# The LSTM steps of a graph and recurrent kernel: where the four gates of a half lie in PSUM, and when each is signalled to ScalarE

## The reference, cut to what matters

```python
x = x + segment_sum(support[src] * w, dst)     # graph layer on layernorm(x); 6250 nodes, 100000 edges
x = x + ffn(layernorm(x))                      # one sequence of 6250 places, 256 features

def step(carry, xp):                           # the LSTM inside ffn, once per place
    h, c = carry
    i, f, g, o = split(xp + h @ W_hh.T, 4)     # 256 columns each
    c = sigmoid(f) * c + sigmoid(i) * tanh(g)
    h = sigmoid(o) * tanh(c)
# after it: a gate per place (argmax of two logits), sums before and after each place,
# 2*h + prefix*fw + suffix*bw
```

## Time and profile before

| | |
|---|---|
| median of 3 runs | 1757.58 us |
| span of the profiled execution | 2362.0 us |
| its own time outside the span | not given |
| plain steps 50 to 113 in it | from 2033.8 us to about 2327 us |
| busy: TensorE, VectorE, GpSimd, ScalarE | 70%, 57%, 49%, 23% of the span |

### The profile page before, as it was taken

How to read it: one execution, slowest core, us unless ns; L and a number is a source line. 1 busy time by engine, 2 the same in 40 slices (tenths; PEclk the granted TensorE clock), 3 DMA queues, 4 the chain that set the end, 5 groups by cost and what they waited for, 6 DMA issues and landing times.

```text
span 2362.0 us, 35522 instructions
## 1 busy us (share of the span) xinstructions
PE 1644.3 (70%) x9417; PEld 1363.5 (58%) x9417; DVE 1357.8 (57%) x4075; ACT 532.0 (23%) x1838; POOL 1166.9 (49%) x1235
## 2 busy tenths in 40 slices
PE   5696766666664576576676676676776776889994
PEld 3385555555552365465565565565565555889993
DVE  8997787777763444344444444444443444556666
ACT  1121000000000022222221222221222222566662
POOL 0377556556545535444444444444344354027774
PEclk9898787878885778777777777787787777999997
DMA  6112222322222223223223223223232233233334
GB/s 169 35 43 61 72 73 68 99 71 73 71 64 80 80 81 93 84 71 95 82 76 95 78 78 94 76 84 93 71 93 84 71 94 101 89 115 114 113 113 131
DMA packets 71694, 202.43 MB, mean 86 GB/s; under 512 B 22785, under 2 KB 25046, under 8 KB 70773
## 3 DMA queue, kind: packets, MB, share of 16 engines
q0 software_dynamic: 48048, 116.84, 18.1%
q1 hardware_dynamic: 23600, 85.04, 11.1%
HBM read 160.49 MB, written 41.17 MB: 85 GB/s over the span
## 4 chain that ended last, share of the span: by engine, by line
PE 45%; issue 20%; DVE 20%; another core or an unknown queue 8%; DVEq 3%; ACT 3%; DMA 0%; POOL 0%; SPq 0%; ACTq 0%
PE bank L1642 14%; PE bank L1616 13%; PE bank L1635 7%; PE bank L1573 5%; PE bank L1540 3%; DVE big_a L999 3%; DVE big_b L1054 2%; DVE big_a L995 2%; DVEq L1057 2%; PE bank L1624 1%; DVE big_c L1048 1%; DVE big_c L997 1%; DVE listed L938 1%; DVE w_ih L938 1%
## 5 line engine op out<-in xcount | busy, mean ns | idle before, releaser
L538 POOL DMA_INDIRECT big_a<-support_scratch,stg_g x636 | 603.8, 949 | 692.2 <-ACT stg_g L618 513.8
L1054 DVE TENSOR_TENSOR big_b<-big_b,bank 125x256 f32 x881 | 367.1, 417 | 663.3 <-remote 396.6
L1642 PE MATMUL bank<-big_c 128*128 128x125 f32 x3648 | 520.8, 287 | 290.7 <-issue 247.9
L1642 PEld LDWEIGHTS bank<-big_c 128*128 128x128 f32 x3648 | 481.2, 199 | 325.4 <-issue 292.2
L1616 PE MATMUL bank<-big_a,big_c 128*125 128x256 f32 x1272 | 474.4, 479 | 122.6 <-issue 94.8
L1616 PEld LDWEIGHTS bank<-big_a,big_c 128*125 128x125 f32 x1272 | 258.6, 239 | 206.8 <-issue 182.4
L1048 DVE TENSOR_SCALAR big_c<-consts_sb,listed 128x125 f32<-128x125 f32 x881 | 308.2, 351 | 76.8 <-issue 49.5
L511 POOL DMA_INDIRECT big_a<-support_scratch,stg_g x245 | 233.9, 955 | 185.3 <-ACT stg_g L618 117.1
L1573 PE MATMUL bank<-big_a,big_c 128*125 128x256 f32 x490 | 171.9, 481 | 151.7 <-issue 91.1
L1635 PEld LDWEIGHTS bank<-xt,w_ih 128*128 128x128 f32 x1600 | 234.6, 213 | 26.0 <-ACT xt L592 10.3
L1635 PE MATMUL bank<-xt,w_ih 128*128 128x125 f32 x1600 | 235.9, 296 | 1.0 <-ACT xt L592 0.8
(11 more groups left out here) (238 smaller groups left out, 1695.0 us busy)
## 6 DMA issues: line engine op xcount, KB each, us to landing
big_c<-gate_input_scratch SPq DMA_DIRECT2D x64, 508.0 KB
gate_input_scratch<-pr SPq DMA_DIRECT2D x50, 508.0 KB
big_a<-support_scratch,stg_g POOLq DMA_INDIRECT x881
support_scratch<-pr SPq DMA_DIRECT2D x12, 448.0 KB
big_b<-in_x SPq DMA_DIRECT2D x2, 1904.0 KB
out<-big_a SPq DMA_DIRECT2D x2, 1456.0 KB
big_b<-in_x SPq DMA_DIRECT2D x1, 1792.0 KB
out<-big_a SPq DMA_DIRECT2D x1, 1344.0 KB
```

Source lines behind the costliest of these rows:

```text
L538: pool.indirect_dma_start(out=ring[:, s, :], out_offset=None, in_=sup_d, in_offset=bass.IndirectOffsetOnAxis(ap=stg_g[:, q, n:n + 1], axis ...
L1054: V.tensor_tensor(at, at, bank[4 + s % PSR][0:SEGS, 0:D], ALU.add).then_inc(added, 1)
L1642: return mm(bank[b + x][:, c * SEGS:(c + 1) * SEGS], w_hh[:, k, g:g + P], h_s[:, q, k, :], start=False, stop=True, skip_group_check=True)
```

## The change

For the plain steps, g leaves the bank of its half. i, f and o stay in the bank 2 - 2q + x (columns 125 to 500), and the two g (half 0 and half 1) share the bank 5 + q. In the far steps sigmoid(o) is written to columns 0 to 125 of the half's own gate bank, where g was. TensorE signals three times for each half: i and f ready (if_r), g ready (g_r), o ready (o_r), and ScalarE waits for each apart. Since ScalarE now reads a bank into which TensorE has still to write, TensorE waits for the reader: for a_if[0] ahead of the last product of o of half 0, for a_g[0] ahead of the last product of g of half 1, for a_if[1] ahead of the last product of o of half 1. `turn_back` is issued ahead of that very last product. Seeds are three copies: both g (250 columns), then i, f, o of each half (375 columns), the latter after h_r[x] of the step before the seeded bank is used anew. Step 49 runs all products in the order k, half, gate. `prefix` uses bank 4 instead of 5. Banks 5 and 6 are written once more before step 49.

```diff
-            def recur(u, q, extra=0, b=None):
-                b = 2 - 2 * q if b is None else b
-                pe.wait_ge(seeded[0], u + 1)
-                pe.wait_ge(seeded[1], u + 1)
+            def recur(u, q, extra=0, back_of=None):
+                pe.wait_ge(seeded_g, u - (SEGL - 1))
+                for x in range(2):
+                    pe.wait_ge(seeded[x], u + 1)
                 pe.wait_ge(h_r[0], u + (extra + 1))
                 for c in (1, 2, 0, 3):
-                    product(q, 0, 0, c, b)
-                for c in (1, 2):
-                    product(q, 0, 1, c, b)
+                    apart(q, 0, 0, c)
+                for c in (0, 1):
+                    apart(q, 0, 1, c)
                 pe.wait_ge(h_r[1], u + (extra + 1))
-                for c in (1, 2, 0, 3):
-                    ins = product(q, 1, 0, c, b)
-                ins.then_inc(g_r[0], 1)
-                for c in (0, 3):
-                    product(q, 0, 1, c, b)
-                for c in (1, 2, 0, 3):
-                    ins = product(q, 1, 1, c, b)
-                ins.then_inc(g_r[1], 1)
+                apart(q, 1, 0, 1)
+                apart(q, 1, 0, 2).then_inc(if_r[0], 1)
+                apart(q, 1, 0, 0).then_inc(g_r[0], 1)
+                for c in (2, 3):
+                    apart(q, 0, 1, c)
+                pe.wait_ge(a_if[0], u + 1)
+                apart(q, 1, 0, 3).then_inc(o_r[0], 1)
+                apart(q, 1, 1, 1)
+                apart(q, 1, 1, 2).then_inc(if_r[1], 1)
+                pe.wait_ge(a_g[0], u + 1)
+                apart(q, 1, 1, 0).then_inc(g_r[1], 1)
+                if back_of is not None:
+                    turn_back(back_of, q)
+                pe.wait_ge(a_if[1], u + 1)
+                apart(q, 1, 1, 3).then_inc(o_r[1], 1)
...
             for x in range(2):
                 pe.wait_ge(xe_r[x], SEGL)
-            for b in (2, 3):
+            pe.wait_ge(added, PSR + TILES)
+            for b in (2, 3, 5, 6):
                 ins = mm(bank[b][:, 0:4 * SEGS], rank_b[:], any_bits, start=True, stop=True)
             ins.then_inc(bits, 1)
-            recur(SEGL - 1, 1, 0, 0)
+            pe.wait_ge(seeded[0], SEGL)
+            pe.wait_ge(seeded[1], SEGL)
+            for k in range(2):
+                pe.wait_ge(h_r[k], SEGL)
+                for x in range(2):
+                    for c in range(4):
+                        ins = product(1, k, x, c, 0)
+                    if k == 1:
+                        ins.then_inc(g_r[x], 1)
```

On ScalarE:

```diff
-            def seed_loaded(u, pair, q, w):
+            def seed_loaded(u, pair, q, w, extra=0):
                 act.wait_ge(xp_l[q], pair * 16 - (SEGL // 2 * 16 - 16))
                 for x in range(2):
                     act.wait_ge(a_o[x], u - 1)
+                given = taken_in[q].rearrange("p (x c) k -> p x c k", x=2)
+                nc.scalar.copy(cell_home(q)[:, 0:2 * SEGS].rearrange("p (x k) -> p x k", x=2),
+                               given[:, :, 0, w:w + SEGS]).then_inc(seeded_g, 1)
                 for x in range(2):
-                    seed_half(q, x, w, 2 - 2 * q, taken_in)
+                    act.wait_ge(h_r[x], u + extra)
+                    nc.scalar.copy(gates_home(q, x)[:, SEGS:4 * SEGS].rearrange("p (c k) -> p c k", c=3),
+                                   given[:, x, 1:4, w:w + SEGS]).then_inc(seeded[x], 1)
...
+            def gates_apart(u, q, x, far):
+                g = gates_home(q, x)
+                i_f, o_g = homes(x, q, far)
+                act.wait_ge(if_r[x], u - (SEGL - 1))
+                nc.scalar.activation(i_f, g[:, SEGS:3 * SEGS].rearrange("p (c k) -> p c k", c=2),
+                                     ACT.Sigmoid).then_inc(a_if[x], 1)
+                act.wait_ge(g_r[x], u + 1)
+                nc.scalar.activation(act_g[:, x, :], cell_home(q)[:, x * SEGS:(x + 1) * SEGS], ACT.Tanh
+                                     ).then_inc(a_g[x], 1)
+                act.wait_ge(o_r[x], u - (SEGL - 1))
+                nc.scalar.activation(o_g, g[:, 3 * SEGS:4 * SEGS], ACT.Sigmoid).then_inc(a_o[x], 1)
```

More of the change, by code:

```diff
@@ L296, in build @@
         seeded = [sem(f"gates_seeded{x}") for x in range(2)]
+        seeded_g = sem("cell_gates_seeded")
         g_r = [sem(f"gates_ready{x}") for x in range(2)]
+        if_r = [sem(f"gates_i_f_ready{x}") for x in range(2)]
+        o_r = [sem(f"gate_o_ready{x}") for x in range(2)]
         a_if = [sem(f"act_i_f_done{x}") for x in range(2)]
@@ L326, in build, with gates_home, cell_home, homes @@
         STORES = (len(LEAVING) - 1) * 32
-        def homes(x, far):
+        def gates_home(q, x):
+            return bank[2 - 2 * q + x]
+        def cell_home(q):
+            return bank[5 + q]
+        def homes(x, q, far):
             if far:
                 return (bank[4][:, x * 2 * SEGS:(x + 1) * 2 * SEGS].rearrange("p (c k) -> p c k", c=2),
-                        bank[5 + x][:, 0:SEGS])
+                        gates_home(q, x)[:, 0:SEGS])
             return act_if[:, x, :, :], act_o[:, x, :]
@@ L676, in seed_loaded, with gates @@
                     act.wait_ge(a_o[x], u - 1)
+                given = taken_in[q].rearrange("p (x c) k -> p x c k", x=2)
+                nc.scalar.copy(cell_home(q)[:, 0:2 * SEGS].rearrange("p (x k) -> p x k", x=2),
+                               given[:, :, 0, w:w + SEGS]).then_inc(seeded_g, 1)
                 for x in range(2):
-                    seed_half(q, x, w, 2 - 2 * q, taken_in)
-            def gates(u, q, x, far, b=None):
-                g = bank[(2 - 2 * q if b is None else b) + x]
-                i_f, o_g = homes(x, far)
+                    act.wait_ge(h_r[x], u + extra)
[12 more added lines that the diff above has]
+                nc.scalar.activation(o_g, g[:, 3 * SEGS:4 * SEGS], ACT.Sigmoid).then_inc(a_o[x], 1)
+            def gates(u, q, x):
+                g = bank[x]
+                i_f, o_g = homes(x, q, False)
                 act.wait_ge(g_r[x], u + 1)
@@ L691, in tanh_c, with step @@
                 nc.scalar.activation(act_c[:, x, :], c_s[:, 1 - q, x, :], ACT.Tanh).then_inc(a_c[x], 1)
[L693 to L697, removed]
+            def step(u, q, far=False):
+                for x in range(2):
+                    gates_apart(u, q, x, far)
+                    tanh_c(u, q, x)
             def take_and_seed(u, q, w):
@@ L717, in place @@
                     for x in range(2):
-                        gates(u, q, x, False, 0)
+                        gates(u, q, x)
                     tanh_c(u, q, 0)
@@ L743, in _ @@
             seed_loaded(SEGL, SEGL // 2, 0, 1)
-            step(SEGL - 1, 1, False, 0)
+            for x in range(2):
+                gates(SEGL - 1, 1, x)
+                tanh_c(SEGL - 1, 1, x)
             seed_loaded(SEGL + 1, SEGL // 2, 1, 1)
@@ L767, in _ @@
                             take_input(j, q, x, j - 1)
+                act.wait_ge(bits, 3)
                 with act.Fori(0, slow_sweeps) as sweep:
@@ L770, in _ @@
                     for q in range(2):
[L771 removed]
+                        seed_loaded(u0 + q, m0, q, 2, sweep)
                     act.sem_inc(ago, 1)
@@ L1382, in finish @@
                 dve.wait_ge(o_v, outputs - 1)
-                link(V.tensor_tensor(base, bank[5][0:SEGS, D:2 * D], bw[0:SEGS, :], ALU.mult))
-                link(V.tensor_tensor(w_even, bank[5][0:SEGS, 0:D], diff, ALU.mult))
+                link(V.tensor_tensor(base, bank[4][0:SEGS, D:2 * D], bw[0:SEGS, :], ALU.mult))
+                link(V.tensor_tensor(w_even, bank[4][0:SEGS, 0:D], diff, ALU.mult))
                 link(V.tensor_tensor(base, base, w_even, ALU.add))
@@ L1643, in product, with apart @@
                           start=False, stop=True, skip_group_check=True)
-            def recur(u, q, extra=0, b=None):
-                b = 2 - 2 * q if b is None else b
-                pe.wait_ge(seeded[0], u + 1)
-                pe.wait_ge(seeded[1], u + 1)
+            def apart(q, k, x, c):
+                g = (4 * x + c) * P
+                home = cell_home(q)[:, x * SEGS:(x + 1) * SEGS] if c == 0 else gates_home(q, x)[:, c * SEGS:(c + 1) * SEGS]
+                return mm(home, w_hh[:, k, g:g + P], h_s[:, q, k, :], start=False, stop=True, skip_group_check=True)
@@ L1664, in place, with turn_back @@
+            def turn_back(n, q):
+                if not isinstance(n, int) or n > 0:
+                    pe.wait_ge(terms_r, n)
+                mm(bank[7][0:SEGS, 0:P + 1], h_s[:, q, 0, :], back[0], start=True, stop=True)
+                mm(bank[7][0:SEGS, P:2 * P + 1], h_s[:, q, 1, :], back[1], start=False, stop=True,
+                   skip_group_check=True).then_inc(back_r, 1)
             def place(it, q):
@@ L1748, in _ @@
             recur(WARM, 0)
-            recur(WARM + 1, 1)
-            turn_back(0, 1)
+            recur(WARM + 1, 1, 0, 0)
             with pe.Fori(1, SEGL // 2) as it:
[L1752 to L1755, removed]
```

(13 more changed lines are left out.)

5 lines of the change are left out of this document (2 added, 3 removed).

## The result

Before 1757.94 us (median of 5 runs), after 1747.76 us (5 runs, 1747.3 to 1750.41). The ratio is 0.9946, interval 0.9935 to 0.9957: 9.5 us saved, against 20.3 forecast. The direction was right, the time lies inside the range, but the gain is under half of what was forecast.

A forecast was written before the change was run, and what follows sets the result against it. The chain from TensorE's first ten products through ScalarE and VectorE to the next step, 4.56 us, was taken as the bound; 63 step starts x 0.33 = 20.8, less 0.5 net, gave 1737.3 us, range 1729.5 to 1750.5.

The forecast's parts named there:

- the last term of the period: TensorE, last o to next step: two loads at 0.11 us; two more waits hidden or costing up to 0.11.
- i and f signalled apart: Start of each plain step: i, f ready after 8 products instead of 10, first sigmoid at 2.13 us instead of 2.58.
- The handshake from ScalarE to TensorE: Held weight loads, such as the last o's: they start 0.05 to 0.11 us after the sigmoid they wait for.
- The rival on the slower side: Weight loads waiting for ScalarE: handshake 0.43 us instead of 0.05, period 4.83, time 1775 us; chance 0.08.
- Half 1 fits by a hair: Half 1's i, f product is ready at 3.57 us, ScalarE free at 3.58, so ScalarE sets the time.
- o behind a wait: Half 0's last product waits for a_if[0]: stream slips about 0.1 us, o ready at 3.13, before tanh(c) at 3.37.
- o in its own bank: Sigmoid of o writing into the bank it reads: taken as no cost; bounds nothing and a doubling, +0.28 us.
- The seeds: ScalarE's three copies instead of two: 1.09 us instead of 1.00, leaving 0.2 us of cover before the next sigmoid.
- Without outputs: Plain steps without outputs: TensorE idles about 0.5 us for a_if[1]; period 4.26 us, gain 0.33 a step.
- The rule of the semaphore increments: TensorE's signals: at 26.3 ns each, four more would add 0.105 us a step, 6.7 us, making 1744; judged unlikely.
- The signs that were named: Trace of plain steps: first sigmoid at 2.1 us, steps 4.2 to 4.3 apart, idle time moved before the last product.
- The first rival: ScalarE or small slips in plain steps take half the gain: period 4.35 to 4.50, 1749 us at 4.42; chance 0.15.

The follow-up runs named there:

- experiment 3: The kernel before the change with TensorE's two loops over the plain steps written out; 1759.1 us, ratio to before 1.0004.
- experiment 1: The changed kernel with TensorE's two loops over the plain steps written out, nothing else touched; 1735.86 us, ratio to before 0.9872.
- experiments 4 and 5: 4: the changed kernel with the turning back behind the last product of o instead of ahead; 1759.3 us, ratio 1.0004. 5 has its own line.
- experiment 5: The changed kernel with TensorE's loops kept, each body begun mid-step behind the product that signals g_r[0]; 1737.35 us, ratio to before 0.9877.

## Why the prediction was wrong

The step that failed is the last term of the period: "the next step's load is due behind them", 0.11 us, with up to 0.11 for two more waits. It counted TensorE's engine instructions and its waits, and not what TensorE's sequencer does between two steps: a branch and register values, which no row of an engine's timeline lists. From the last o's first load to the next step's it reckoned two loads at 0.11, with that allowance 0.22 to 0.33. In one step in two it is 0.30, which the term covers. In the other it is 0.64: 0.34 more, and 0.37 in the steps without outputs. The trace has 23 such intervals with outputs and 6 without (the last pass of a loop does not go back), and 0.2 us more at the loops' ends: 23 x 0.34 + 6 x 0.37 + 0.2 = 10.2 us. From the first sigmoid of step 50 to that of step 113 the kernel after takes 277.7 us and experiment 3 288.0. So 10.3 us are gained in the traces, where 20.8 were forecast, and 20.8 - 10.2 = 10.6; the timed runs have 9.5 (7.6 to 11.4). The prediction said of the two new waits that they "can hide behind the last two matmuls". Two matmuls are 0.22 us; the branch, which it did not count, is 0.21 alone.

The other steps, point by point:
- *i and f signalled apart*: right. From a step's first load to its sigmoid it is 2.09 us (1607.14 to 1609.23), where 2.13 was forecast. In experiment 1 the interval is 4.18 with outputs, between the 4.17 and 4.23 of the text.
- *The handshake from ScalarE to TensorE*: sigmoid of half 1 ends at 1601.85 + 0.36 = 1602.21, the load it holds begins at 1602.26. That is 0.05, the low bound. The rival on the slower side falls with it.
- *Half 1 fits by a hair*: right; its sigmoid starts 1.46 after that of half 0 (1600.39, 1601.85), as before.
- *o behind a wait*: right. Sigmoid of o waits for TensorE (0.38 us) and tanh(c) still follows in time (1602.78, 1603.08).
- *o in its own bank*: nothing, as taken. 259 ns by the group below, where the earlier trace rows had 276.

```profile
L704 ACT ACTIVATE bank<-bank 128x125 f32<-128x125 f32 x99 | 25.6, 259 | 38.3 <-PE bank L1676 38.3
```

- *The seeds*: 1603.29 to 1604.45, 1.16 us where 1.09 was reckoned, and 0.19 us of idle time behind them even in the short step: cover as reckoned. In experiment 1 they end 0.11 us before the next sigmoid, which starts 2.09 behind the step's first load as in the kernel after; so they don't bind there either, but the margin is small.
- *Without outputs* TensorE was to idle about 0.5 us for a_if[1]: 0.49. And here the way back is open too:

```profile
1465.70 0.30 PEld L1676 LDWEIGHTS bank<-big_c 128*128 128x128 f32 x2 [0.49 <-ACT big_c L698]
1466.34 1.75 PEld L1676 LDWEIGHTS bank<-big_c 128*128 128x128 f32 x15 [0.34 <-issue]
```

- *The rule of the semaphore increments*: seven increments a step cost nothing that could be found. Experiment 1 has all of them and steps of 4.18, less than the 4.23 taken without the rule.
- *The signs that were named*: "I am wrong if the releaser of a step's first product is still h[0]". It is not; but issue was not among the signs, and it is what the trace shows. The first rival, "small slips take half of it", names the size of the result, and not its cause: ScalarE's margins held.

The prediction knew that TensorE would become nearly full and that a new wait would stand two matmuls before its step's end. What the sequencer does between two steps should then have been listed beside the matmuls that can cover it.

## What to carry to other kernels

Ahead of a change that puts a wait near the end of a loop's body, find when the last wait ahead of the loop's end is met, list what the sequencer does from there to the next pass (branch, register values, waits), and count the queued work that is left to cover it: here 0.64 us against 0.22 us of matmuls. A wait that is met long before its turn, as the turning's was before the change, does no harm. If the cover is too little, begin the body elsewhere in the period or write the loop out; both gave back more than the change itself had (12 and 13 us by the ratios, against 9.5). An alternation of long and short periods with the loop's own period is the sign of it.

## What the runs showed of the hardware

- TensorE's COMPARE_BRANCH takes 0.21 us when it goes back and 0.08 in a loop's last pass; the whole way back left the weight loads idle for 0.34 us. It costs nothing with enough matmuls queued: the kernel before gains nothing when it is written out (experiment 3), and in experiments 4 and 5 the loads keep their pace. The Trainium skill, Advanced Engine Details and Errata, section "Control Flow Timing", gives about 108 ns for a compare and branch; the trace has 208.
- A wait that isn't met holds back the loop's instructions behind it: they start 0.04 us after a_if[1] is signalled in the kernel after (31 of 31 passes), 0.05 after terms_r before (24 of 24), 0.05 to 0.06 after h[1] in experiment 5 (29 of 29). With 20 loads between wait and loop's end it was 0.39 (the loop without outputs before, 7 of 7). The page just named, section "Sequencer Loop", lists semaphore readiness as something the engine instruction waits for after it was pushed into the queue. Read so, the branch would be free to run ahead of an unmet wait; in the passes counted here it never does.
- From the end of ScalarE's sigmoid to the start of the weight load that waited for it: 0.05 us.
